# Where VectorE's one-off setup work stands in the first attention phase, and where ScalarE's table with the tanh is loaded

## The reference

```python
x = x + 0.5 * _L0_ffn_ref(_layernorm(x), ...)    # attention of 16 heads of width 8, layer norm, router, 4 experts, layer norm
x = x + _L0_attn_ref(_layernorm(x), ...)         # retention: 8 heads, rotary q and k, decay mask, group norm, gate, projection
x = x + 0.5 * _L0_ffn_ref(_layernorm(x), ...)    # same weights as the first
```

## Time and profile before

| what | us |
|---|---|
| median of 3 runs | 995.02 |
| lowest and highest run | 992.1, 999.49 |
| the profiled execution's own time | 995.09 |
| its span in the trace | 993.3 |

### The profile page before, as it was taken

How to read it: one execution, slowest core, us unless ns; L and a number is a source line. 1 busy time by engine, 2 the same in 40 slices (tenths; PEclk the granted TensorE clock), 3 DMA queues, 4 the chain that set the end, 5 groups by cost and what they waited for, 6 DMA issues and landing times.

```text
span 993.3 us, 26905 instructions
## 1 busy us (share of the span) xinstructions
PE 889.4 (90%) x8698; PEld 658.8 (66%) x8698; DVE 768.1 (77%) x1934; ACT 685.3 (69%) x1398; POOL 615.7 (62%) x915
## 2 busy tenths in 40 slices
PE   8799999999997989799999998899999999997883
PEld 5566666666656885567777776566666666666883
DVE  5788888888978785466666667688888888978775
ACT  3688888888884773245555555788888888874773
POOL 4245757575746676467777777236666575655666
PEclk9799999999999999999999999899999999998997
DMA  9994796000045772200000000000000000046571
GB/s 296 387 415 69 224 406 269 11 17 15 17 133 176 204 236 67 65 1 1 0 0 0 0 1 1 2 2 13 21 11 21 11 21 11 23 131 196 170 246 45
DMA packets 36678, 97.69 MB, mean 98 GB/s; under 512 B 4633, under 2 KB 20271, under 8 KB 31997
## 3 DMA queue, kind: packets, MB, share of 16 engines
q1 hardware_dynamic: 31100, 84.16, 25.7%
q0 software_dynamic: 5504, 12.63, 3.6%
HBM read 44.68 MB, written 53.13 MB: 98 GB/s over the span
## 4 chain that ended last, share of the span: by engine, by line
PE 44%; issue 19%; DVE 18%; POOL 12%; DMA 3%; ACT 2%; DVEq 1%; SPq 1%; POOLq 0%; ACTq 0%
DVE mx L1430 9%; PE duo L592 7%; PE duo L648 7%; POOL out L2034 3%; PE duo L585 3%; DVE qk_lo L1419 2%; POOL x_mid L2034 2%; PE duo L657 2%; PE duo L888 2%; POOL xs L2019 2%; PE duo L959 2%; PE duo L899 2%; PE duo L586 1%; PE duo L743 1%; PE duo L874 1%
## 5 line engine op out<-in xcount | busy, mean ns | idle before, releaser
L1430 DVE TENSOR_REDUCE mx<-duo 128x4 fp32r<-128x1024 f32 x256 | 312.2, 1219 | 60.8 <-PE duo L592 55.1
L1132 ACT ACTIVATE probs<-duo 128x1024 f32<-128x1024 f32 x256 | 263.2, 1029 | 59.0 <-PE duo L598 55.2
L592 PE MATMUL duo<-stacks 32*128 32x256 f32 x1024 | 129.7, 330 | 34.1 <-DVE mx L1430 28.4
L648 PE MATMUL duo<-probs,v_st 128*32 128x256 f32 x2048 | 139.1, 390 | 0.3
L598 PE MATMUL duo<-q_st,stacks 32*128 32x256 f32 x1024 | 129.8, 331 | 0.1
L592 PEld LDWEIGHTS duo<-stacks 32*128 32x128 f32 x1024 | 78.1, 185 | 71.5 <-issue 29.3
L1923 POOL TENSOR_TENSOR a_ln<-mv_ln,eps_ln 128x2 f32<-128x2 f32 x32 | 6.3, 196 | 145.0 <-DVE mv_ln L1395 144.9
L585 PE MATMUL duo<-qk_hi,sel_r 128*128 128x256 f32 x256 | 79.8, 334 | 7.2 <-DVE qk_lo L1419 7.2
L743 PE MATMUL duo<-w,xs 128*128 x608 | 78.7, 285 | 7.3 <-ACT xs L1163 4.4
L1771 DVE TENSOR_TENSOR ret<-duo,dm 128x768 f32<-128x768 f32 x64 | 61.0, 953 | 30.6 <-PE duo L878 27.7
L648 PEld LDWEIGHTS duo<-probs,v_st 128*32 128x32 f32 x2048 | 53.9, 110 | 41.1 <-issue 2.0
(11 more groups left out here) (238 smaller groups left out, 2424.3 us busy)
## 6 DMA issues: line engine op xcount, KB each, us to landing
x_sorted<-ret SPq DMA_DIRECT2D x2, 17476.0 KB, 53.3
wall<-w_pack SPq DMA_DIRECT2D x38, 578.0 KB
ret<-x_sorted SPq DMA_DIRECT2D x22, 257.0 KB
stacks<-x_sorted SPq DMA_DIRECT2D x12, 257.0 KB
w_pack<-wall SPq DMA_DIRECT2D x2, 1024.0 KB, 6.1
decay_rows<-prow SPq DMA_DIRECT2D x1, 1536.0 KB
xs<-x_sorted SPq DMA_DIRECT2D x4, 257.0 KB
rows<-in_c_sel_ffn SPq DMA_DIRECT2D x1, 1024.0 KB, 7.1
```

The lines of the kernel that those rows point to most:

```text
L592: return pe.matmul(score_bank[h % 2][:, t * SEQ:(t + 1) * SEQ], q_st[r:r + 32, g, t * P:(t + 1) * P], k_st[r:r + 32, g, :], start=True, st ...
L648: last = pe.matmul(pv_bank[32 * j:32 * j + 32, cols], v_st[:, t, h, :], probs[:, h % RING, t, :], start=(t == 0), stop=(t == TT - 1))
L1132: act.activation(probs[:, h % RING:h % RING + 2, :, :], duo_now[:].rearrange("p (n t q) -> p n t q", n=2, t=TT), ACT.Exp, scale=SCALE).the ...
L1430: dve.tensor_reduce(rows, score_duo[:].rearrange("p (n t k) -> p n t k", n=2, t=TT), AX.X, ALU.max, negate=True).then_inc(max_done, 1)
```

## The change

Half 1 of the expert weights is packed in batch 2 instead of batch 1, one expert at a time (slots 2, 4, 6 and 7). The selectors' rounding is cut into two halves in two slots. Parts 3 and 4 move one slot or two on. Parts 5 to 13 go from slots 2 to 6 of batch 1 to slots 6 and 7 of batch 1 and slots 0 and 1 of batch 2. On ScalarE a set with the name `exp_and_others` is asked for right after the first experts stage, ahead of retention's first wait.

```diff
@@ ScalarE, after the first experts stage
             experts(0, attend)
+            act.preload_act_table_set("exp_and_others")
             retain, attend = retention(), phase(BATCH)
@@ VectorE, later_setup
-                    dve.tensor_copy(sel2_r[:].rearrange("p g k m -> p (g k m)"), dm_flat[:, 0:2048]).then_inc(set_dve, 1)
+                    dve.tensor_copy(sel2_r[:].rearrange("p g k m -> p (g k m)")[:, 0:1024], dm_flat[:, 0:1024])
                 elif part == 3:
+
+                    dve.tensor_copy(sel2_r[:].rearrange("p g k m -> p (g k m)")[:, 1024:2048], dm_flat[:, 1024:2048]).then_inc(set_dve, 1)
+                elif part == 3.5:
@@
-            LATER_PARTS = 14
+            LATER_AT = {(1, 1): (2,), (1, 2): (3,), (1, 3): (3.5,), (1, 4): (4,), (1, 6): (5, 6, 7), (1, 7): (8, 9),
+                        (2, 0): (10, 11), (2, 1): (12, 13)}
@@ VectorE, phase
-                        if isinstance(i, int) and i == 1 and p in (1, 2):
-                            (pack_hi, pack_lo)[p - 1](1)
-                        if isinstance(i, int) and i == 1 and 1 <= p <= 6:
-                            later_setup(2 * p)
-                            later_setup(2 * p + 1)
+                        if isinstance(i, int):
+                            for part_no in LATER_AT.get((i, p), ()):
+                                later_setup(part_no)
+                        if isinstance(i, int) and i == 2 and p in (2, 4):
+                            pack_hi(1, range(p // 4, p // 4 + 1))
+                        if isinstance(i, int) and i == 2 and p in (6, 7):
+                            pack_lo(1, range(p - 6, p - 5))
```

## The result

Over 20 runs of each kernel, taken in turns, the changed kernel takes 988.57 us in the median against 996.6 before; the ratio is 0.9933, with a 95% interval from 0.9908 to 0.9957. The profiled execution took 990.25 us with a span of 988.4, 4.8 us less than the 995.09 of before. The medians are of all runs; the ratio leaves out those more than 1.5% above the fastest run of the same kernel, four of the kernel before and none of the changed one.

The account below looks back on a forecast made before the run. Attention was taken as a VectorE-TensorE ping-pong in which batch 1's setup is not hidden, costing wait, work and clock. Gains of 4.3 (batches 1 and 2), 1.0 (table) and 1.7 (clock) made 7.0: 995.09 to 988.1 us, range 984.5 to 993.5.

Parts of the forecast that it names:

- the clock behind the table: Start of retention, behind the first tanh: with less idle time TensorE's clock would not fall, 1.7 us; falling anyway, 0.30.
- Batches 1 and 2: First two attention batches: moving pack and setup work out of batch 1 would gain 4.3 us, between 1.7 and 6.7.
- a best case of 32.1 us and a worst of 37.1: Batches 1 and 2 together: VectorE's extra work hidden beside TensorE's at best, or added in full at worst; before, 38.84.
- The shares of 0.90 and 0.87 from the routing batches: VectorE's busy shares of batches 3 and 4; applied to batches 1 and 2 they gave 35.0 to 36.2 us.
- the three prices: Unhidden setup in batch 1 was said to cost three times: VectorE's store wait, its work, and TensorE's lower clock.
- The wait for the seven loads: Batch 1, setup part 2 on VectorE, now ahead of the store's wait: taken as 0, at most 1.2 us.
- The queues: Later hand-over of powers and pack to the DMA queues: no price; the first clearing has 6.1 us until GpSimd waits.
- The rival's mechanism: Rival, batch 3: GpSimd waits for the first clearing, which cuts attention's gain at 6.1 us; 986.3 us, chance 0.03.
- GpSimd beside the packs: Batch 2: two subtractions on VectorE slow GpSimd's chain by 0.6 us, hidden by 4.5 us of idle time per batch.
- The table: ScalarE at retention's first tanh: without the table load there the tanh starts earlier, 1.0 us, bounds 0 and 1.28.
- the rival of repeated loads: Rival, retention's loop: the set asked for lacks a function, so 15 further table loads; 1006.8 us, chance 0.04.
- the mechanism of the prediction: Start of retention: TensorE's idle time at the table load makes its clock fall to 1.2 GHz behind the tanh.

Follow-up runs that it names:

- the fill: Kernel before, plus 13 matrix products without use that keep TensorE busy in the gap of batch 1's slot 3: 999.39 us, ratio 1.0037.
- pack only: Kernel before, with only the pack of half 1 moved to batch 2 and the other setup left in place: 1000.24 us, ratio 1.0031.
- setup only: Kernel before, with setup parts 2 to 13 spread as in the change, half 1 still packed in batch 1, no table asked for: 993.22 us, ratio 0.997.
- the second trace: The changed kernel run again without any edit: 989.54 us, ratio 0.995 to the kernel before.
- the late clearing: Changed kernel, with the first clearing issued only after the maxima of slot 2 of batch 1: 996.0 us, ratio 1.0006 to the kernel before.
- no fill: Sets apart a run of VectorE's part only plus 7 matrix products without use at the first tanh: 989.13 us, ratio 0.9943.
- the last run: Changed kernel, with the first clearing issued ahead of the bias store and 20 instead of 17 fill products ahead of retention: 988.62 us, ratio 0.9931.

## Why the prediction was right, and what it had wrong in its steps

The time, 988.1 forecast and 988.57 measured, was right; against the medians of before, 995.02 then and 996.6 over 20 runs, the gain was 7.0 forecast and 8.0 measured, and 6.7 by the ratio (0.67% of 996.6). That the sum is within 0.5 us of the median is in part luck. The batches were put 1.6 us too low, and the clock behind the table was booked with 1.7 us of which at most a part is sure. What the stretches show for the two parts whose causes hold, 5.9 + 1.0 = 6.9 us, agrees with the 6.7 of the ratio.

**Batches 1 and 2: 4.3 forecast, 5.9 measured.** The place and the causes were right: no wait for the store, no lower clock, batch 2 hardly longer. The size was off because I took the middle between a best case of 32.1 us and a worst of 37.1 (which is 34.6, so 4.2 and not 4.3). VectorE's busy time, forecast at 15.2 and 16.3 us, came out at 15.61 and 15.73. The trace shows 32.94, close to the best: batch 2 hid 2.7 us of new busy time (15.73 - 12.99) at a price of 0.4. The shares of 0.90 and 0.87 from the routing batches were the wrong rows to lean on; VectorE reaches 15.61 / 16.71 = 0.93 and 15.73 / 16.23 = 0.97 with its extra work spread in pieces of 0.4 to 0.8 us. Of the three prices only the clock's was measured by itself: 1.9 us, by the fill. The wait was 1.13 us in this trace and 0.42 and 0.53 in two others. What is left of the 5.9, 2.9 us, would be the work's; no run takes the wait or the work away alone. Undoing either half of VectorE's part leaves 3.6 us (pack only) or 1.8 us (setup only) of the gain lacking, and the lower clock is in the first of these and not in the second.

**The wait for the seven loads: 0 forecast, 0 measured.** The rounding starts at 33.14, right behind the clearing of the small tiles.

**The queues: nothing forecast, nothing measured for the powers; the clearing nearly bound.** The powers' store is issued at 50.62 and the masks' loads at 108.25, against 51.21 and 108.59. I gave the clearing 6.1 us of slack and a chance of 0.03 as the bound. In the first trace the scatter came 5.7 us earlier (78.51 against 84.20) and the clearing landed 0.6 us later (78.7 against 78.1), so the slack was used up: GpSimd waited 0.15 us by the merged ticks, and 0.21 us in the second trace, where the clearing landed at 79.3. In three further traces with the same VectorE part it waited 0.04 us or less. The rival's mechanism is real, as the late clearing shows; its chance was too small since the main term was sized too small.

**GpSimd beside the packs: 0.6 us of growth forecast, hidden.** GpSimd's busy time in batch 2 went from 6.41 to 6.95, by 0.54, and the idle time ahead of its chain stayed at 144.1 / 32 = 4.5 us. GpSimd's timeline of the changed kernel shows where:

```profile
59.55 0.73 POOL L1960 TENSOR_TENSOR rows<-token_bufs,vecs_sb 128x256 f32<-128x256 f32 x1
60.24 1.19 POOL L1971 TENSOR_TENSOR rows<-xs,vecs_sb 128x256 f32<-128x256 f32 x1
```

The second sum has the size of the first and takes 0.46 us longer; VectorE's subtraction runs from 60.15 to 60.83 beside it. The Trainium skill's rule (GPSIMD Engine Reference, Specifications) holds in kind, with a fifth of the 2.2 us that it would have allowed. In all seven traces with the pack in batch 2 this sum stands beside the subtraction and takes 1.18 to 1.21 us; no GpSimd instruction beside the second subtraction was slowed by as much. So the growth of 0.5 us is near the 0.6 forecast, but it is one sum that was slowed and not two normalisations.

**The table: 1.0 us forecast, 1.0 measured.** Kernels in which the clock held in retention's first 30 us take 199.6 and 199.7 us with the load at the tanh, and 198.6, 198.7 and 198.6 without. No further load appeared, so the rival of repeated loads fell. The drain of 1.38 us that the Trainium skill (ScalarE: Activation LUTs, What ACT_TABLE_LOAD costs) adds to a load would have made this 2.4; the stretches show 1.0.

**The clock behind the table: 1.7 us forecast, present in the first trace, not a sure gain.** The retention stage was indeed 2.6 us shorter in the first pair, and the idle time at the tanh did shrink by most of its length (1.51 to 0.47 us). What failed is to book 1.7 us as a term on that. TensorE has three waits of over a microsecond near the start of retention, and every one of the nine falls of the clock there, in all twelve traces, began within 1.6 us of the end of one of them:

| TensorE's wait | length, us | traces with it | a fall behind it |
|---|---|---|---|
| for the first batch | 1.24 to 1.92 | 11 | 3 |
| at the tanh, with the load there and no fill | 1.50 to 1.52 | 6 | 3 |
| for GpSimd, some 8 us later | 1.36 to 1.39 | 12 | 3 |

Without the load the wait at the tanh is 0.46 to 0.48 us, and in none of these five traces did a fall begin there. That fits the mechanism of the prediction, but three of six against none of five is little to go by, and the change leaves the other two waits as they were. A fall of 3.4 us cost about 1.6 us (with the load, 201.1 to 201.3 us against 199.6 and 199.7). By these counts the change saves half of that, some 0.8 us, on average; this is an estimate. The means agree: retention took 201.0 us with the load (those six traces) and 199.4 without (five), a difference of 1.6, of which 1.0 is the load itself. Whether the other 0.6 is due to the change, these few traces do not settle.

**What was lost again in the first trace** was the 2.6 us in the experts stage, and it went with the clock. TensorE spent 6.8 us of that stage at the lower level in the first trace of before and 10.2 in that of the changed kernel. Over all twelve traces the stage took 107.6 and 108.4 us where it spent none there, 109.9 at 3.4, 109.1 to 110.5 at 6.8, and 110.0 to 111.8 at 10.2 or more. It took 109.1 to 111.8 us in the six kernels whose VectorE part was not, or only in part, as in the change, and 107.6 to 111.7 in the other six; there is no sign of the change in it.

## What to carry to other kernels

One-off setup in a pipelined loop can cost more than its busy time: batch 1 became 6.3 us shorter when 2.8 us of VectorE's busy time left it, with the wait for a store and the lower clock, and the rest was spread; the next batch took the same 2.7 us of work, in pieces of 0.4 to 0.8 us, for 0.4. No run puts the moved work into the next batch in lumps, so how much the pieces matter there stays open. Before such a gain is booked, look at what has a fixed time of its own, like a long transfer that is issued early; here GpSimd reaches the clearing with no slack left in two traces of five, and any further gain ahead of it would be cut; issued 4 to 6 us later, the clearing cost all of the gain. A gain that consists in a clock level not falling should stand in the sum as a chance and not as a term, and be told from a cut of the trace by stages, since a span varies by more than such a gain.

## What was not expected of the hardware

An idle gap of TensorE did not decide alone whether its clock fell: in batch 1 it fell behind 1.75 us once and held through 1.65 and 1.51 us in a row another time, and of the 29 waits of 1.24 to 1.92 us near the start of retention 9 brought it down. The same stage with the same work differed by 4.2 us from trace to trace (107.6 to 111.8), roughly in step with the time at the lower level. A GpSimd sum of 128x256 took 1.18 to 1.21 us beside a subtraction on VectorE, in seven traces out of seven, and 0.73 or 0.74 us without it. The small bias store (8 KB) took 2.2 to 2.3 us on SP's queue in three traces and 0.46 or 0.47 in eight. The clearing behind it was then issued some 1.8 us later but took 47.3 to 47.8 us to land instead of 49.1 to 49.8, so its landing hardly moved. Issued right behind the clearing, in the last run, the same store held the queue for 23.35 us.
